# Masks of the FFN's seven-product groups: by transposing DMAs and additions instead of small matmuls

## What is computed

```python
inter = xf @ c1_w.T @ c2_w.T                    # scores, rank 16
blk = inter.reshape(B * T, n_blocks, SPARSITY)  # 56 blocks of 64
idx = jnp.argmax(blk, axis=-1) + jnp.arange(0, INTER, SPARSITY)
w1_g = w1[idx]
w2_g = w2t[idx]
h = jax.nn.relu(jnp.einsum('bkm,bm->bk', w1_g, xf))
out = jnp.einsum('bk,bkm->bm', h, w2_g)
```

## Time and profile before

| | us |
|---|---|
| Three runs | 787.74, 787.85, 789.07 |
| Median | 787.85 |
| Profiled execution: span from the first to the last instruction | 785.8 |

### The profile page before, as it was taken

The page is one execution under the profiler, slowest core; times in us unless marked ns, Lnnn a source line. Parts: engine busy times, 40 slices in busy tenths (PEclk is TensorE's granted clock), DMA queues, the critical chain, the costliest instruction groups (busy, mean ns, idle before and its releaser), DMA issues.

```text
span 785.8 us, 11435 instructions
## 1 busy us (share of the span) xinstructions
PE 778.8 (99%) x3859; PEld 640.2 (81%) x3864; DVE 608.9 (77%) x968; ACT 245.1 (31%) x368; POOL 443.4 (56%) x269
## 2 busy tenths in 40 slices
PE   8999999999999999999999999999999999999998
PEld 7888886578888888888888888888888888888886
DVE  6888769878884878787878778787888787777864
ACT  6348666963321130303121221203031212212030
POOL 4887898567999953545444352535454544525240
PEclk9999999999999999999999999999999999999999
DMA  9436411000111110111111111111011111111104
GB/s 329 187 116 214 157 50 59 8 2 6 61 54 61 53 57 18 46 55 53 60 53 60 53 60 53 60 52 30 31 53 60 53 60 53 60 53 53 53 21 192
DMA packets 22758, 55.30 MB, mean 70 GB/s; under 512 B 4560, under 2 KB 6608, under 8 KB 22480
## 3 DMA queue, kind: packets, MB, share of 16 engines
q1 hardware_dynamic: 22592, 53.96, 19.8%
q10 hardware_dynamic: 144, 1.05, 0.3%
HBM read 50.79 MB, written 4.19 MB: 70 GB/s over the span
## 4 chain that ended last, share of the span: by engine, by line
PE 97%; DVE 1%; ACT 1%; DMA 0%; issue 0%
PE bank L1843 13%; PE bank L1844 13%; PE bank L1845 13%; PE bank L1739 12%; PE bank L1741 12%; PE bank L1740 12%; PE bank L1539 4%; PE bank L1541 4%; PE bank L1540 4%; PE bank L1691 4%; PE bank L1730 2%; PE bank L1555 1%; PE bank L1709 1%; PE bank L1748 1%; PE bank L1756 1%; PE bank L1678 0%
## 5 line engine op out<-in xcount | busy, mean ns | idle before, releaser
L1843 PE MATMUL bank<-w_hi,h_hi 128*128 128x512 f32 x448 | 175.1, 391 | 0.0
L1844 PE MATMUL bank<-w_lo,h_hi 128*128 128x512 f32 x448 | 174.9, 390 | 0.0
L1845 PE MATMUL bank<-w_hi,h_lo 128*128 128x512 f32 x448 | 174.3, 389 | 0.0
L1331 DVE TENSOR_TENSOR x<-bank,x 128x512 f32<-128x512 f32 x208 | 133.4, 684 | 50.0 <-PE bank L1845 50.0
L600 POOL TENSOR_TENSOR lo_r<-r,slot 128x512 fp32r<-128x512 f32 x52 | 67.4, 1297 | 155.3 <-ACT slot L832 155.3
L1845 PEld LDWEIGHTS bank<-w_hi,h_lo 128*128 128x128 f32 x448 | 84.1, 188 | 17.9
L1843 PEld LDWEIGHTS bank<-w_hi,h_hi 128*128 128x128 f32 x448 | 84.1, 188 | 16.2
L1844 PEld LDWEIGHTS bank<-w_lo,h_hi 128*128 128x128 f32 x448 | 84.3, 188 | 15.5
L1739 PE MATMUL bank<-xT_hi,slot 128*128 128x512 f32 x240 | 94.9, 396 | 0.0
L1740 PE MATMUL bank<-xT_lo,slot 128*128 128x512 f32 x240 | 93.4, 389 | 0.0
L1741 PE MATMUL bank<-xT_hi,lo_r 128*128 128x512 f32 x192 | 74.9, 390 | 0.0
(11 more groups left out here) (215 smaller groups left out, 1605.6 us busy)
## 6 DMA issues: line engine op xcount, KB each, us to landing
r<-w SPq DMA_DIRECT2D x56, 256.0 KB, 3.5
w_raw<-w SPq DMA_DIRECT2D x28, 512.0 KB, 4.0
x<-x_in SPq DMA_DIRECT2D x8, 512.0 KB, 10.5
ctx_raw<-ctx_in SPq DMA_DIRECT2D x8, 512.0 KB, 3.3
xn<-ctx_in SPq DMA_DIRECT2D x8, 512.0 KB, 4.5
out<-x SPq DMA_DIRECT2D x7, 512.0 KB, 2.6
W_raw<-wqkv SPq DMA_DIRECT2D x6, 512.0 KB, 10.4
xT_raw<-xT_in SPq DMA_DIRECT2D x1, 2048.0 KB, 20.4
```

The lines of the kernel that those rows point to most:

```text
L1331: nc.vector.tensor_tensor(x[:, t, c], bank[unit_banks(g)[p]][:, :], x[:, t, c], ALU.add).then_inc(unit_added, 1)
L1843: nc.tensor.matmul(dst, h_hi[:, j, m], w2_hi[:, j, c], start=j == 0, stop=False)
L1844: nc.tensor.matmul(dst, h_hi[:, j, m], w2_lo[:, j, c], start=False, stop=False)
L1845: last = nc.tensor.matmul(dst, h_lo[:, j, m], w2_hi[:, j, c], start=False, stop=j == GJ - 1)
```

## The change

In the fast groups no matmul adds a mask. The picks are written with the subtraction score x order - maximum, where `order` now holds multiples of 2^120: 0 for the picked unit, at most -2^120 for the others. For the fast groups they go to `pick_pair`, two buffers of a pair of tiles each. A transposing DMA of SyncE's queue (`turn_mask`) turns each pair, 128x512 in bf16, into `mask_T`, with the units on the partitions: four a group. Two are issued in the output stage of the group before, behind the loads of r and c2, and two behind the loads of w2, each once its pair of picks is there. Three of the four masks are added by GpSimd to operands of the block sums (`add_mask`: to p1 for c11, to u4 for c12, to u7 for c21), the fourth by VectorE in c22; v22 is now made in bank 1. For this the lists of GpSimd and ScalarE change order (the cuts of w2 move), product 5 counts in `hid_done` instead of `prod_done`, and the last two products open their banks themselves. The plain groups keep their mask matmuls, with the bf16 identity. `floor_b` goes; `order` is scaled once by GpSimd.

```diff
+PICK_STEP = 2.0 ** 120
+PRODS, MASKED = 3, 3
+    pick_pair = at("pick_pair", 196, [P, 2, 2, GH], BF16)
+    mask_T = [at("mask_T0", 198, [P, TB, GJ, P], BF16), at("mask_T1", 150, [P, TB, GJ, P], BF16)]
+        u4_masked = p1
...
+            def turn_mask(g, n):
+
+                sp.wait_ge(pick_ready, g * PAIRS + (n + 1))
+                sp.sem_inc(turning, 1)
+                half = slice(2 * (n % 2), 2 * (n % 2) + 2)
+                sp.dma_start_transpose(mask_T[n // 2][:, half, :, :].rearrange("p t r m -> p (t r) m"),
+                                       pick_pair[:, n % 2, :, :].rearrange("p t h -> p (t h)")
+                                       ).then_inc(mask_loaded[n], 16)
...
                     sp.wait_ge(c2_done, g + 2)
                     load_c2(g + 2)
+                if masks:
+                    sp.wait_ge(masked, fast(g + 1, MASKED, -1))
+                    turn_mask(g + 1, 0)
+                    turn_mask(g + 1, 1)
                 sp.wait_ge(unit_done, g * NU + NU)
                 for j in range(GJ):
                     load_w2(g + 1, j)
+                if masks:
+                    turn_mask(g + 1, 2)
+                    turn_mask(g + 1, 3)
...
+            nc.gpsimd.tensor_scalar(order[:, :], order[:, :], PICK_STEP, 0.0, ALU.mult, ALU.add).then_inc(order_ready, 1)
...
+            def add_mask(g, dst, part, r, b):
+
+                for n in range(2):
+                    pool.wait_ge(mask_loaded[2 * b + n], (g - PLAIN) * 16 + 16)
+                nc.gpsimd.tensor_tensor(by_tile(dst), by_tile(part), mask_of(r, b), ALU.add).then_inc(masked, 1)
...
                 lo_A(g, 3, r12, slot0, lo_r12)
+                lo_w2(g, 0)
                 lo_A(g, 4, r21, slot1, lo_r21)
-                lo_w2(g, 0)
+                pool.wait_ge(sum_done, summed(g, "u2"))
+                add_mask(g, p1, p1, 0, 0)
                 lo_A(g, 5, r11, slot2, lo_r11)
+                pool.wait_ge(sum_done, summed(g, "c11"))
+                add_mask(g, u4_masked, u4, 0, 1)
+                lo_A(g, 6, r22, slot0, lo_r22)
+                pool.wait_ge(sum_done, summed(g, "u7"))
+                add_mask(g, u7, u7, 1, 0)
                 lo_w2(g, 1)
-                lo_A(g, 6, r22, slot0, lo_r22)
...
                 hi_A(g, 3, r12, slot0)
-                act.wait_ge(prod_done, fast(g, 4, 1))
+                hi_w2(g, 0)
+                act.wait_ge(prod_done, fast(g, PRODS, 1))
                 act.wait_ge(comb_done, fast(g, 4, 2))
                 hi_A(g, 4, r21, slot1)
-                hi_w2(g, 0)
-                act.wait_ge(prod_done, fast(g, 4, 2))
+                hi_w2(g, 1)
+                act.wait_ge(prod_done, fast(g, PRODS, 2))
                 act.wait_ge(comb_done, fast(g, 4, 3))
                 hi_A(g, 5, r11, slot2)
-                hi_w2(g, 1)
...
-                nc.vector.tensor_tensor(pk, sc, first, ALU.not_equal).then_inc(pick_ready, 1)
+                if not plain and n >= 2:
+                    dve.wait_ge(mask_loaded[n - 2], (g - PLAIN) * 16 + 16)
+                elif not plain and not (isinstance(g, int) and g == PLAIN):
+                    dve.wait_ge(mask_loaded[n + 2], (g - PLAIN) * 16)
+                nc.vector.tensor_tensor(pk, sc, first, ALU.subtract).then_inc(pick_ready, 1)
...
             def make_c11(g):
                 dve.wait_ge(hid_done, g * 4 + 1)
+                dve.wait_ge(masked, fast(g, MASKED, 0))
                 add_sum(bank[4][:, :], 4, p1)
...
             def make_c12(g):
                 dve.wait_ge(hid_done, g * 4 + 3)
-                add_sum(bank[2][:, :], 2, u4)
+                dve.wait_ge(masked, fast(g, MASKED, 1))
+                add_sum(bank[2][:, :], 2, u4_masked)
...
             def make_c22(g):
-                dve.wait_ge(hid_done, g * 4 + 2)
                 dve.wait_ge(sum_done, summed(g, "v22"))
-                add_sum(bank[1][:, :], 1, v22)
+                for n in (2, 3):
+                    dve.wait_ge(mask_loaded[n], (g - PLAIN) * 16 + 16)
+                nc.vector.tensor_tensor(by_tile(bank[1][:, :]), by_tile(bank[1][:, :]), mask_of(1, 1),
+                                        ALU.add).then_inc(sum_done, 1)
...
-                product(bank[4][:, :], slot0, lo_r12, B21, True)
-                hidden_mask(g, 0, 0)
-                pe.wait_ge(sum_done, summed(g, "u4"))
-                hidden_mask(g, 1, 1, alone=True)
-                opening_mask(g, 0, 1)
-                pe.wait_ge(p1_copied, fast(g, 1, 0))
-                opening_mask(g, 1, 0)
+                product(bank[4][:, :], slot0, lo_r12, B21, True, True).then_inc(hid_done, 1)
                 hidden_bank(g, 3)
                 cut_ready(4)
                 pe.wait_ge(T_lo_done, 8)
-                product(bank[3][:, :], slot1, lo_r21, (T_hi[3], T_lo[3]), True, True).then_inc(prod_done, 1)
+                product(bank[3][:, :], slot1, lo_r21, (T_hi[3], T_lo[3]), True, True).then_inc(hid_done, 1)
                 cut_ready(5)
-                product(bank[2][:, :], slot2, lo_r11, B22, False, True).then_inc(hid_done, 1)
+                pe.wait_ge(sum_done, summed(g, "u4"))
+                product(bank[2][:, :], slot2, lo_r11, B22, True, True).then_inc(hid_done, 1)
```

More of the change, by code:

```diff
@@ L31 @@
 WARM = 44
-FLOOR = -2.0 ** 120
+PICK_STEP = 2.0 ** 120
 ROUND = 12582912.0
@@ L115, in decoder_layer @@
     SB = TB * P
+    PAIRS = NT // 2
     SCALE = 1.0 / 16.0
@@ L259, in decoder_layer @@
         id_b_ready = sem("id_b_ready")
+        order_counted = sem("order_counted")
         order_ready = sem("order_ready")
@@ L315, in decoder_layer @@
         T_lo_done = sem("T_lo_done")
-        floor_ready = sem("floor_ready")
+        mask_loaded = [sem(f"mask_loaded{n}") for n in range(PAIRS)]
+        turning = sem("turning")
+        masked = sem("masked")
         c2_done = sem("c2_done")
@@ L359, in decoder_layer @@
         NU = 2 * NT
-        PAIRS = NT // 2
         def cuts_before(g):
@@ L405, in decoder_layer, with mask_of, by_tile @@
         u2, p1 = sums[:, 0, 0, SB:], sums[:, 1, 0, SB:]
-        v22 = sums[:, 1, 1, SB:]
+        u4_masked = p1
+        def mask_of(r, b):
+            return mask_T[b][:, :, r, :]
+        def by_tile(part):
+            return part.rearrange("p (t m) -> p t m", t=TB)
         block = ctx.enter_context(nc.Block())
@@ L465, in _, with next_group @@
             load_c2(1)
-            def next_group(g, last):
+            def turn_mask(g, n):
[5 more added lines that the diff above has]
+                                       ).then_inc(mask_loaded[n], 16)
+            def next_group(g, last, masks=True):
                 sp.wait_ge(hid_done, g * 4 + 4)
@@ L477, in next_group @@
                     load_w2(g + 1, j)
-            with sp.Fori(0, NG - 2) as g:
+                if masks:
+                    turn_mask(g + 1, 2)
+                    turn_mask(g + 1, 3)
+            for g in range(PLAIN - 1):
+                next_group(g, False, masks=False)
+            with sp.Fori(PLAIN - 1, NG - 2) as g:
                 next_group(g, False)
@@ L648, in _ @@
             nc.gpsimd.iota(order[:, :], pattern=[[-1, BLK]], base=BLK, channel_multiplier=0,
-                           allow_small_or_imprecise_dtypes=True).then_inc(order_ready, 1)
+                           allow_small_or_imprecise_dtypes=True).then_inc(order_counted, 1)
+            pool.wait_ge(order_counted, 1)
+            nc.gpsimd.tensor_scalar(order[:, :], order[:, :], PICK_STEP, 0.0, ALU.mult, ALU.add).then_inc(order_ready, 1)
             for t in range(6):
@@ L856, in copy_p1 @@
             def copy_p1(g):
-                act.wait_ge(prod_done, fast(g, 4, 0))
+                act.wait_ge(prod_done, fast(g, PRODS, 0))
                 nc.scalar.activation(p1, bank[0][:, :], ACT.Copy).then_inc(p1_copied, 1)
@@ L874, in hi_h @@
                     act.wait_ge(sum_done, summed(g, f"c{r + 1}{b + 1}"))
+                    if (r, b) == (1, 1):
+                        act.wait_ge(masked, fast(g, MASKED, 1))
                 nc.scalar.activation(h_hi[:, r, b * SB:(b + 1) * SB], bank[c_bank(g, r, b)][:, :],
@@ L1255, in pick_first @@
                 sc = score_bank[n % 2][:, :].rearrange("p (b w) -> p b w", w=BLK)
-                pk = pick[:, 2 * i:2 * i + 2, :].rearrange("p t (b w) -> p (t b) w", w=BLK)
+                plain = isinstance(g, int) and g < PLAIN
+                pk = pick[:, 2 * i:2 * i + 2, :] if plain else pick_pair[:, n % 2, :, :]
+                pk = pk.rearrange("p t (b w) -> p (t b) w", w=BLK)
                 wide = [P, BANK // BLK, BLK]
@@ L1280, in make_u2 @@
                 dve.wait_ge(p1_copied, fast(g, 1, 0))
-                dve.wait_ge(prod_done, fast(g, 4, 2))
+                dve.wait_ge(prod_done, fast(g, PRODS, 2))
                 add_sum(u2, 1, p1)
@@ L1291, in make_c11 @@
                 dve.wait_ge(hid_done, g * 4 + 1)
+                dve.wait_ge(masked, fast(g, MASKED, 0))
                 add_sum(bank[4][:, :], 4, p1)
```

(31 more changed lines are left out.)

4 lines of the change are left out of this document (removed).

## The result

In the comparison made for this result the changed kernel takes 776.45 us in the median of 4 runs (775.73 to 776.57), the kernel before 788.17 (787.74 to 789.07). The ratio is 0.9847, with a 95% interval of 0.9835 to 0.9858: 11.7 us faster. The forecast was 775.7, with a range of 774.6 to 784.0.

A forecast was written before the change was run, and what follows sets the result against it. TensorE's own instructions were taken to bound the kernel. Removing the masks takes 12 x 1.01 = 12.1 us off 787.85, with the added work priced at nothing: 775.7, range 774.6 to 784.0.

The forecast's parts named there:

- What bounds the kernel and what goes: TensorE alone sets the pace; dropping 192 mask matmuls wins 1.01 us in each of 12 groups, 12.1 us.
- VectorE: Same sums and prices, position against TensorE kept; c22 begins at 15.2 after the group's start, limit 16.2: no cost.
- GpSimd: Three mask adds a group at 1.30 us each; second w2_lo ends 0.8 us before its use: priced at nothing, narrowest cover.
- the limit for the turn: Latest harmless landing of a group's last transposing DMA, set by GpSimd's work behind it: 13.2 us after the group's start.
- ScalarE: The w2_hi move ahead of two slot copies; the first ends near 5.3 us after the group's start: costs nothing.
- SyncE and the turn: Four transposing DMAs a group, each landing in 2.0 to 5.2 us, taken as 3.5; the last lands at 11.4, in time.
- Outside the groups: Scaling of `order` on GpSimd comes, scaling of the identity on VectorE goes: between -0.3 and +0.3 us, taken as 0.
- Rival A: Turns of 5.2 us in series land 1.6 late, TensorE waits for w2_lo 1.6 us a group: 794.9; chance 0.14.
- Rival B: GpSimd's mask adds make w2_lo late, half the gain: at 2.0 us an add 782.9; chance 0.12, partial waits included.
- m: Time of one GpSimd mask add; the second w2_lo ends at 16.3 + 2m, so TensorE waits from m = 1.7 us.
- Rival C: The time of the masks was hidden or comes back in full as another wait: no change, 787.9; chance 0.04.

The follow-up runs named there:

- another order: Changed kernel with the cuts of w2 put back where the kernel before has them in the lists of GpSimd and ScalarE: 791.03 us, ratio 1.0038.
- three turns in a row: Changed kernel with the last transposing DMA of each group done three times in series: 798.91 us.
- the late wide turn: Changed kernel with two transposing DMAs of 128x1024 a group instead of four of 128x512, the late one issued when pick 3 is there: 775.71 us.
- the doubled adds: Changed kernel with all three mask adds of GpSimd done twice in each group: 798.34 us.
- the kernel with a single small wait: Changed kernel with GpSimd's last mask add of each group (on u7) done twice: 781.3 us, ratio 0.9912.
- the kernel with single blocks: Changed kernel with each transposing DMA cut into four of one 128x128 block, sixteen a group: 808.25 us.

## Why the prediction was right

**What bounds the kernel and what goes:** right. The price of the masks read from the starts, 1.01 us a group, is 1.01 by the kernel without them, and 0.985 of it is won in the changed one. The forecast's 12.1 us are so 0.3 too many. The busy times of the earlier trace rows give 17.2 us for all 224 mask matmuls, 14.7 for the 192, and would have been 25% off.

**VectorE:** right in that it costs nothing; its position was not quite kept. Picks 2 and 3 end at 4.49 and 8.01, 0.09 later. u2 starts at 8.36 and c11 at 12.06; the latter is 0.37 later than I placed it, because the first cut of c2 takes 0.90 us instead of 0.54, and harmless. c22 starts at 15.52 instead of 15.2, before the limit of 16.2. The third h_lo ends 0.37 ahead of the outputs, where I had it keep 0.47; why is open.

**GpSimd:** the path and its order were right, the sizes on the safe side. The add costs 1.13 between starts (I took 1.30 of the range 1.07 to 1.30), and neighbouring operations overlap by 0.05. So the limit for the turn is 13.8 instead of 13.2. That w2_lo's margin came out near the forecast, 0.95 for 0.8, is partly luck: the second add began 0.44 later than 12.4, as c11 was late, and the work behind it took 5.95 instead of 6.5. It is the narrowest cover on GpSimd, as said (the cut of product seven has 1.04): one add more costs 5 us, another order 15. In time h_lo's 0.37 on VectorE is narrower, and no experiment lengthened that path.

**ScalarE:** right. The first w2_hi ends at 4.99, and the slot copy behind it starts at 5.72 as in the kernel before.

**SyncE and the turn:** right by the range, and the value taken, 3.5 us, too high: 2.4, between 2.0 of 16 KB and 3.5 of 256 KB. What I had no term for is the time that SyncE is held by the issue (a part of the 2.4): 1.2 us, three times a plain DMA's 0.42. With four turns a group it does not matter, since SyncE has nothing else due then, and the w2 loads are issued 0.19 after the outputs end as before; with sixteen it decides.

**Outside the groups:** right. From group 0 to group 1 it is 52.07 us against 52.08, to group 2 45.57 in both.

**Rival A** (late turns): a late turn does cost TensorE time, but the kernel is 3.3 us away from it. With three turns in a row, 1.7 past the measured limit, a group loses 1.86 us (798.9 in all); the rival had 1.6 for a landing 1.6 past its own, without the extra of a wait. It put the wait at w2_lo, and it stands at product seven; and it let the second turn queue behind the first, while the runs show two under way together. The 5.2 us a turn of this rival agrees with the estimate in the prediction from the figure of 1309 ns a block in the Trainium skill's page VectorE: DVE Perf Modes (The three transpose paths). By that figure, if it were a rate, the late wide turn would take 10.5 us; it takes 3.0. So here it is no rate for each block, and as the price of a single block it is lower than the one measured, 2.3 from the start of the issue to the landing. The Trainium skill's page Advanced Engine Details and Errata (X-Bar Transpose) calls such DMAs as fast as regular ones; for the landing this holds here within what can be seen (128 KB turned land in 2.4 us, 16 KB plain in 2.1, 256 KB plain in 3.5; but the plain ones come from DRAM and the turned ones from SBUF, and no run has both from one place), for the issue not.

**Rival B** (GpSimd late): excluded by the price of 1.17 for the mixed add, but the doubled adds show what it would have cost: 22 us at m = 2.3, where my line gives 14 at that m. The line had no wait ahead of product seven and no extra for a wait.

**Rival C** (no change): excluded, for the same reason as the two others; TensorE has no idle time in any group.

The difference of 0.75 us between the forecast and the median is made up of 0.3 from the kernel before (788.17 in this comparison, 787.85 in the one that I started from) and 0.4 from the gain (11.7 instead of 12.1).

## What to carry to other kernels

When TensorE has no gap, the price of small matmuls is read from the starts around them, not from their busy time, and here it was all won, since the replacement landed on engines that have room at that very place. Whether it has room is decided by the order of the list on the engine that takes the work, read against due times, not by its share of busy time: GpSimd at 62% had 0.95 us to spare, and with two operations in the old order the same change made the kernel slower. Turn many blocks in one transposing DMA where the issuing queue is short of time: it is held for about 1.2 us by each, with one block or eight. Where it is not, the number makes no difference: two, four and eight DMAs a group gave 775.71, 776.45 and 776.16.

## What the runs showed that was not expected

**A wait costs TensorE more than its length.** In these traces, behind waits from 0.3 to 2.4 us, the first step is 0.33 to 0.34 us instead of 0.23, and in the kernel with a single small wait the loss is 0.47 for 0.32 of lateness. (A wait is told here as the lateness against the undisturbed start; the idle time in the rows is 0.16 shorter.)

**Its clock can drop behind a wait of 2 us.** In the kernel with single blocks, three of the twelve groups lost more than the others, two of them 1.5 us, the first 2.6 (its wait was 3.1 us long instead of 2.0). The first of them, one of the other two and a regular group, by stretches (length; busy us and count of PE, PEld, DVE, ACT and POOL; granted clock, DMA share and GB/s), and a few matmuls of the second:

```profile
289.50:293.50 4.00, 3.95 (x11) 3.17 (x12) 0.86 (x2) 0.14 (x1) 3.44 (x2) 0.61 0.00 0
420.00:423.20 3.20, 1.38 (x7) 0.80 (x5) 2.15 (x4) 1.10 (x2) 2.42 (x3) 1.00 0.00 0
423.20:426.50 3.30, 3.29 (x8) 2.62 (x9) 0.82 (x2) 0.10 (x1) 3.30 (x2) 0.54 0.00 0
466.50:468.80 2.30, 0.46 (x3) 0.04 (x1) 1.74 (x3) 1.11 (x2) 2.30 (x3) 1.00 0.00 0
468.80:472.00 3.20, 3.19 (x14) 2.62 (x15) 0.82 (x3) 0.09 (x1) 3.20 (x2) 1.00 0.00 0
```

```profile
420.99 0.39 PE L1796 MATMUL bank<-xT_hi,lo_r 128*128 128x512 f32 x1
423.21 0.58 PE L1794 MATMUL bank<-T_hi,slot 128*128 128x512 f32 x1 [1.84 <-POOL lo_r L631]
423.59 0.63 PE L1795 MATMUL bank<-T_lo,slot 128*128 128x512 f32 x1
...
426.96 0.39 PE L1794 MATMUL bank<-T_hi,slot 128*128 128x512 f32 x1
```

After the wait of 2.0 us that ends at 423.21, the mean granted clock of the stretch is 0.54 of full speed: nearly all of it is at the lower level, 1.2 GHz. The matmuls step by 0.43 us instead of 0.23 until 426.96. After a wait of the same length that ends at 468.81 it stays at 1.00. Of the eleven waits of 2.0 us in this trace two are followed by the lower level, and so is the one of 3.1; the 1.7 us waits of the kernel with three turns never were, and one of 2.4 us there was not either. So the length of the wait alone does not decide it in these traces; what does stays open. For the change it means that a replacement that is late by 2 us can lose more than the lateness.
